# Fused weight products of the second attention: from sixteen steps ahead of the first attention to eight pieces inside it

## The reference

```
x = x + L0_attn(layernorm(x))   # 16 heads of 16, window of 64, a gated memory MLP and a SwiGLU FFN
x = x + L0_ffn(layernorm(x))    # relu MLP plus a weighted expert
x = x + L1_attn(layernorm(x))   # latent attention, 16 heads of 128
x = x + L1_ffn(layernorm(x))    # mixture of 16 experts, top 6, plus a shared one
```

```
c_kv = h @ W_DKV.T + b          # 64 wide
c_q  = h @ W_DQ.T + b           # 192 wide
q = c_q @ W_UQ.T + b ; k = c_kv @ W_UK.T + b ; v = c_kv @ W_UV.T + b    # 16 heads of 128
scores = q_h k_h^T / sqrt(128) ; out = concat_h(softmax(scores) v_h) @ W_O.T + b_O
```

## Time and profile before

| | |
|---|---|
| Time of before, median of 3 runs | 744.55 us (741.0 to 757.64) |
| Profiled execution, span | 757.9 us |
| PE busy | 691.1 us, 91% |
| DVE, ACT, POOL busy | 413.2, 329.3, 262.8 us |
| Chain that ended last: PE's share | 78% |
| Mean granted TensorE clock | 0.935 |

### The profile page before, as it was taken

One profiled execution on the slowest core, in us unless ns is written; L12 is line 12 of the kernel. 1 busy time (PEld: TensorE's weight loads), 2 busy tenths in 40 slices (PEclk: granted clock), 3 DMA queues, 4 the chain that ended last, 5 costly groups with the idle time before them and its releaser, 6 DMA issues.

```text
span 757.9 us, 13212 instructions
## 1 busy us (share of the span) xinstructions
PE 691.1 (91%) x5202; PEld 562.9 (74%) x5202; DVE 413.2 (55%) x870; ACT 329.3 (43%) x780; POOL 262.8 (35%) x340
## 2 busy tenths in 40 slices
PE   2979999899988699978689999799999999999997
PEld 1655767677777578866577777677888888888886
DVE  6566485833434766454836464566553454545455
ACT  2232535433533334444577687578442323232322
POOL 4313241602143650440732543235314334333400
PEclk9988889866889889998999999899999999999999
DMA  5322200000011220000200000000044433343201
GB/s 191 114 71 56 67 3 2 5 26 1 2 50 42 64 62 1 22 22 1 63 1 1 23 1 1 2 2 1 3 119 118 128 112 97 102 131 109 69 30 55
DMA packets 18636, 37.31 MB, mean 49 GB/s; under 512 B 2544, under 2 KB 4720, under 8 KB 18576
## 3 DMA queue, kind: packets, MB, share of 16 engines
q1 hardware_dynamic: 18576, 36.48, 16.0%
HBM read 35.19 MB, written 1.11 MB: 48 GB/s over the span
## 4 chain that ended last, share of the span: by engine, by line
PE 78%; DVE 9%; ACT 6%; POOL 3%; issue 3%; DMA 1%; DVEq 0%; SPq 0%; ACTq 0%; POOLq 0%
PE ps L632 50%; PE ps L945 4%; PE ps L957 4%; PE ps L751 3%; PE ps L935 3%; PE ps L775 3%; PE ps L710 2%; PE ps L654 2%; PE ps L658 1%; PE ps L640 1%; PE ps L725 1%; PE ps L649 1%; PE ps L693 1%; DVE st L1310 1%; DVE sml L1638 1%
## 5 line engine op out<-in xcount | busy, mean ns | idle before, releaser
L1841 POOL TENSOR_SCALAR PB<-PB,sml 128x256 f32<-128x256 f32 x128 | 60.2, 490 | 88.8 <-DVE sml L1655 88.8
L1151 ACT CAST VVh<-U 128x512 fp32r<-128x512 f32 x50 | 31.1, 621 | 114.3 <-DVE U L1512 106.6
L632 PE MATMUL ps<-ATh,wh 128*128 128x512 f32 x176 | 72.0, 409 | 3.6 <-POOL wl L1812 2.1
L632 PE MATMUL ps<-ATh,wl 128*128 128x512 f32 x176 | 70.9, 403 | 0.0
L632 PE MATMUL ps<-ATl,wh 128*128 128x512 f32 x176 | 70.8, 403 | 0.0
L1810 POOL TENSOR_SCALAR wh<-wr 128x768 fp32r<-128x768 f32 (+3 forms) x31 | 25.8, 833 | 129.0 <-PE ps L632 124.3
L1504 DVE TENSOR_TENSOR U<-U,ps 128x512 f32<-128x512 f32 x50 | 34.4, 688 | 62.5 <-PE ps L632 60.9
L1222 ACT ACTIVATE PB<-ps,sml 128x256 f32<-128x256 f32 x128 | 59.3, 487 | 8.8 <-DVE sml L1649 8.8
L1812 POOL TENSOR_TENSOR wl<-wr,wh 128x768 fp32r<-128x768 f32 (+3 forms) x31 | 56.0, 1806 | 2.6
L1516 DVE TENSOR_TENSOR VVl<-U,VVh 128x512 fp32r<-128x512 f32 x50 | 35.9, 718 | 37.1 <-ACT VVh L1151 37.1
L945 PE MATMUL ps<-SM,PB 128*128 128x128 f32 x256 | 37.8, 290 | 9.1 <-DVE QHl L1298 7.2
(11 more groups left out here) (294 smaller groups left out, 2050.0 us busy)
## 6 DMA issues: line engine op xcount, KB each, us to landing
wr<-in_w SPq DMA_DIRECT2D x32, 384.0 KB, 3.1
wr<-in_w SPq DMA_DIRECT2D x16, 321.0 KB, 2.9
CB<-weights_of_experts SPq DMA_DIRECT2D x16, 256.0 KB, 3.9
wr<-in_w SPq DMA_DIRECT2D x11, 256.0 KB, 2.6
CB<-weights_of_experts SPq DMA_DIRECT2D x8, 224.0 KB, 3.6
CB<-weights_of_experts SPq DMA_DIRECT2D x8, 192.0 KB, 3.7
CB<-weights_of_experts SPq DMA_DIRECT2D x8, 160.0 KB, 3.6
XO<-in_x SPq DMA_DIRECT2D x2, 512.0 KB, 4.7
```

Of the source, the lines that this page charges most:

```text
L632: t = x.matmul(o, a, b, start=first and i == 0 and c == 0, stop=last and i == n - 1 and c == 2, skip_group_check=skip)
L1151: x.copy((VV if run == "moe" else HH)[c][0][:, :], b[:, :]).then_inc(*mark("hi", "h", run, j, half))
L1841: t = x.tensor_scalar(p[:, c, :], p[:, c, :], m[:, 16 + c:17 + c], 1.0, ALU.mult, ALU.mult)
```

## The change

- `PROLOGUE`, `PERIOD` and `LAST` become one written list `FIRST`. With the `fuse`, `spin` and bias items taken out, the items of PE, ACT and DVE stand there in the same order as before, apart from `l0begin` and items that issue nothing. On POOL the splits of `wo` and `mem0` move from the end of the prologue to where `mem1` and `mem2` were split, so that four stand in a row.
- `fuse j` is now a piece of two heads, eight pieces in all. Pieces 0 and 1 stand among the scores of sequence 0; 2, 4 and 6 follow `expo 0 0`, `expo 1 0` and `expo 2 0`; 3, 5 and 7 follow `score 1 1`, `score 2 1` and `score 3 1`. Both halves k share one bank `fm`. ACT and DVE evacuate each piece right where it stands.
- The banks `fm` and `fn` come from the ring `w`, which has four banks from the start, and the scores have both pairs from the start. `l0begin` is gone.
- The 16 bias matmuls go. DVE adds up `bout` over the heads with 16 instructions (`biases j`), and one matmul with a column of ones sums over the partitions (`bias`).
- Both `spin` items (12 and 2 matmuls) go. The loads of `wr` wait for the bias sum too.

```diff
-        ring = {"w": Turns((6, 7)), "m": [Turns((2,)), Turns((3,))], "n": Turns((4,)), "S": Turns((8,))}
+        ring = {"w": Turns((4, 5, 6, 7)), "S": Turns((9, 8))}
...
+        def fuse(j):
+            bm, bn = fills(ring["w"], "fm", j), fills(ring["w"], "fn", j)
+            for i in range(2):
+                raw = raw_of(f"fuse{2 * j + i}")
+                uq, uk, uv, wo_ = raw[:, 0:256], raw[:, 256:321], raw[:, 321:385], raw[:, 386:642]
+                e.wait_ge(*loaded(f"fuse{2 * j + i}"))
+                x.matmul(bm[:, i * 65:i * 65 + 65], uq[:, 0:128], uk, start=True, stop=True)
+                t = x.matmul(bn[64 * i:64 * i + 64, 0:256], uv, wo_, start=True, stop=True)
+                if i:
+                    t.then_inc(*filled("fn", j))
+                t = x.matmul(bm[:, 130 + i * 65:130 + i * 65 + 65], uq[:, 128:256], uk, start=True, stop=True)
+            t.then_inc(*filled("fm", j))
+
+        def bias():
+            b = fills(ring["w"], "fb")
+            e.wait_ge(*at("biased", 15))
+            e.wait_ge(*at("ones"))
+            x.matmul(b[:, 0:256], ON[:, 16:17].to_broadcast([128, 128]), bout[:, :], start=True, stop=True).then_inc(
+                *filled("fb"))
...
+        def fuse(j):
+            lo_part(("fn", j), NTW[1][:, j, :], bank("fn", j)[:, 0:256], NTW[0][:, j, :])
+            (mh, rh), (ml_, rl) = fused_of(j)
+            vm, vr = fused_in(j)
+            e.wait_ge(*at("hi", "fm", j))
+            x.tensor_tensor(ml_, vm, mh.bitcast(F32), ALU.subtract)
+            x.tensor_tensor(rl, vr, rh.bitcast(F32), ALU.subtract).then_inc(*vacates("fm", j))
+
+        def biases(j):
+            for h in (2 * j, 2 * j + 1):
+                raw = raw_of(f"fuse{h}")
+                e.wait_ge(*loaded(f"fuse{h}"))
...
+                    e.wait_ge(*at("biased", h - 1))
+                    x.scalar_tensor_tensor(out=bout[:, :], in0=raw[:, 386:642], scalar=raw[:, 385:386], in1=bout[:, :],
+                                           op0=ALU.mult, op1=ALU.add).then_inc(*mark("biased", h))
...
                 if before.startswith("fuse"):
-                    e.wait_ge(*at("fused", int(before[4:])))
+                    e.wait_ge(*have("fm", int(before[4:]) // 2))
+                    e.wait_ge(*have("fn", int(before[4:]) // 2))
+                    e.wait_ge(*at("biased", int(before[4:])))
```

More of the change, by code:

```diff
@@ L142 @@
     _in[PART[_n]] = _n
-PROLOGUE = [
[15 rows of a table removed]
-]
-PERIOD = [
[9 rows of a table removed]
-]
-LAST = [
[6 rows of a table removed]
-    "mlpwide", "step@a mem 2 0", "split mem4", "oproj@p 5", "oproj@a 4", "step@a mem 3 0", "step@p mem 3 0",
[20 rows of a table removed]
-    "step@v ffn 2 1", "split exp", "split down", "ffnturn@v 0", "step@p ffn 3 1", "ffnturn@a 0", "step@a ffn 3 1",
[3 rows of a table removed]
-    "down ffn 4 1", "down ffn 5 1", "split proj", "latnorm 0", "latturn@v 0", "l1begin@v", "ffnmean@v 1", "latturn@a 0",
[13 rows of a table removed]
+FIRST = [
[61 rows of a table added]
+    "step@v ffn 1 1", "ffnnorm@a 0", "down@p ffn 1 1", "split@g exp", "step@a ffn 2 1", "step@v ffn 2 1", "ffnturn@p 0",
+    "split@g down", "step@p ffn 3 1", "ffnturn@a 0", "ffnturn@v 0", "step@a ffn 3 1", "down@p ffn 2 1", "step@v ffn 3 1",
[16 rows of a table added]
 ]
@@ L255, in split @@
             if LEFT[n] is not None and not done.get(LEFT[n]):
-                return
-            if n in ("wo", "mem0") and not state.get("fused"):
                 return
@@ L305, in mlp @@
         return tail[1]
-    for text in PROLOGUE:
-        kind, *a = text.split()
-        if kind == "split":
-            state["fused"] = True
-            split()
-        else:
-            item(kind, *map(int, a))
-    for b in range(3):
-        for text in PERIOD:
-            kind, d, k = text.split()
-            if kind == "spin":
-                item(kind, int(d))
-                continue
-            name, d, k = kind.partition("@")[0], int(d), int(k)
-            if b + d > 3 or b + d < 0 or d == 2 and b == 2:
-                continue
-            if name in ("project", "rope", "finish", "turnqk"):
-                item(kind, 2 * (b + d) + k)
-            elif name in ("headnorm", "turnmx"):
-                item(kind, b + d)
-            elif name not in ("weighed", "parted") or b + d >= 0:
-                item(kind, b + d, k)
-        if b == 1:
-            done["qkv0"] = done["qkv1"] = True
-            split()
-    for text in LAST:
+    for text in FIRST:
         kind, *a = text.split()
@@ L535, in half_cols, with fused_of, fused_in @@
         return slice(half * 512, half * 512 + 512)
+    def fused_of(j):
+        return [(m[:, :, j * 128:j * 128 + 128].rearrange("p k (h c) -> p k h c", c=64), r[:, :, 2 * j:2 * j + 2])
+                for m, r in zip(MTW, RTW)]
+    def fused_in(j):
+        v = bank("fm", j)[:, 0:260].rearrange("p (k h c) -> p k h c", k=2, c=65)
+        return v[:, :, :, 0:64], v[:, :, :, 64]
     def tile_cols(t):
@@ L641, in turn @@
             t.then_inc(*filled(*key))
-        def fuse(h):
-            raw = raw_of(f"fuse{h}")
-            uq, uk, uv, wo_ = raw[:, 0:256], raw[:, 256:321], raw[:, 321:385], raw[:, 386:642]
-            e.wait_ge(*loaded(f"fuse{h}"))
-            for k in range(2):
-                b = fills(ring["m"][k], "fm", h // 4, k) if h % 4 == 0 else bank("fm", h // 4, k)
-                t = x.matmul(b[:, (h % 4) * 65:(h % 4) * 65 + 65], uq[:, k * 128:(k + 1) * 128], uk, start=True, stop=True)
-                if h % 4 == 3:
-                    t.then_inc(*filled("fm", h // 4, k))
-            b = fills(ring["n"], "fn", h // 2) if h % 2 == 0 else bank("fn", h // 2)
-            lo = 64 * (h % 2)
-            t = x.matmul(b[lo:lo + 64, 0:256], uv, wo_, start=True, stop=True)
-            if h % 2:
-                t.then_inc(*filled("fn", h // 2))
-            b = fills(5, "fb") if h == 0 else bank("fb")
-            x.matmul(b[:, 0:256], raw[:, 385:386].to_broadcast([128, 128]), wo_, start=h == 0, stop=h == 15).then_inc(
-                *mark("fused", h))
+        def fuse(j):
[16 more added lines that the diff above has]
+                *filled("fb"))
         def turn1(half):
@@ L695, in turnqk @@
                 i.then_inc(*filled(key, t))
-        def l0begin():
-            ring.update(S=Turns((9, 8)), w=Turns((4, 5, 6, 7)))
-            for s in (vacated("fm", 3, 0), vacated("fm", 3, 1), vacated("fn", 7), vacated("fb")):
-                e.wait_ge(*s)
         def l0last():
@@ L893, in latconst @@
             e.wait_ge(*vacated("la", half, 2))
-            e.wait_ge(*vacated("fm", 3, 1))
+            e.wait_ge(*vacated("fm", 7))
             mm3(b[0:16, :], [((RTW[0][:, k, :], RTW[1][:, k, :]), (BT[0][:, k, sl], BT[1][:, k, sl]))
@@ L965, in l1out @@
             e.wait_ge(*vacated("lw", i))
+            e.wait_ge(*vacated("fn", j))
             for qt in range(2):
@@ L994, in spread @@
             p.then_inc(*filled("sp", half))
-        run(order, "p", {"spin": spin, "consts": consts, "fuse": fuse, "turn1": turn1, "project": project, "turnqk": turnqk, "l0begin": l0begin,
+        run(order, "p", {"spin": spin, "consts": consts, "fuse": fuse, "turn1": turn1, "project": project, "turnqk": turnqk, "bias": bias,
                     "score": score, "turnmx": turnmx, "expo": expo, "weigh": weigh, "oproj": oproj,
@@ L1029, in norm1 @@
                     x.copy(parts[k][0][:, 0:832], raw_of(f"qkv{k}")[:, 0:832]).then_inc(*mark("hi", f"qkv{k}"))
-        def fuse(h):
-            if h % 2:
-                hi_part(("fn", h // 2), NTW[0][:, h // 2, :], bank("fn", h // 2)[:, 0:256])
-            if h % 4 == 3:
-                j = h // 4
-                for k in range(2):
-                    v = bank("fm", j, k)[:, 0:260].rearrange("p (h c) -> p h c", c=65)
-                    e.wait_ge(*have("fm", j, k))
-                    x.copy(MTW[0][:, k, j * 256:j * 256 + 256].rearrange("p (h c) -> p h c", c=64), v[:, :, 0:64])
-                    x.copy(RTW[0][:, k, 4 * j:4 * j + 4], v[:, :, 64]).then_inc(*mark("hi", "fm", j, k))
+        def fuse(j):
+            hi_part(("fn", j), NTW[0][:, j, :], bank("fn", j)[:, 0:256])
+            (m, r), (vm, vr) = fused_of(j)[0], fused_in(j)
+            e.wait_ge(*have("fm", j))
+            x.copy(m, vm)
+            x.copy(r, vr).then_inc(*mark("hi", "fm", j))
         def turn(key, to, half, k, scale=None):
@@ L1376, in consts, with fuse, bias @@
                 *mark("slt"))
-        def fuse(h):
-            if h % 2:
-                j = h // 2
-                lo_part(("fn", j), NTW[1][:, j, :], bank("fn", j)[:, 0:256], NTW[0][:, j, :])
-            if h % 4 == 3:
-                j = h // 4
-                for k in range(2):
-                    v = bank("fm", j, k)[:, 0:260].rearrange("p (h c) -> p h c", c=65)
-                    mh, ml_ = (m[:, k, j * 256:j * 256 + 256].rearrange("p (h c) -> p h c", c=64) for m in MTW)
-                    e.wait_ge(*at("hi", "fm", j, k))
```

(22 more changed lines are left out.)

## The result

| | before | after |
|---|---|---|
| Timed median of the first comparison (4 runs each) | 748.84 us | 782.96 us (780.73 to 791.09) |
| Ratio, 95% interval | | 1.053 [1.041, 1.064] |
| Profiled execution, span | 757.9 us | 782.5 us |
| Mean granted clock | 0.935 | 0.915 |

The changed kernel is slower, by 34 us where 18.6 were predicted (763.0); 783 lies above the range, which ended at 775. The ratios leave out executions that were slow beside the others of the same kernel, the medians hold them all. On the two profiled executions the difference is 24.6 us, and it comes to 34 in the medians, since the profiled execution of before was a long one.

The account below looks back on a forecast made before the run. PE was taken to bound the periods, other engines' latency the emptied prologue. After 13.9 us gained, 5 were left at `project 4`; -5 + 10.4 + 4.8 + 4.5, 2.4 and 1.5 for clock gave +18.6: 763.0 us, range 748 to 775.

Parts of the forecast that it names:

- Milestones and waits: Start times from `project 0` to `project 4`, and new PE waits of 2.6, twice 3.1 and 1.85 us with named releasers.
- The half clock assumed for `project 0`: Prologue start: PE has done little by then, so the first projection takes 4.2 us at half clock.
- The first rival: New waits for DVE are hidden: 10.7 us fall away, +8, 752.5 us; chance 0.22.
- Pieces and waits at full clock: Periods and `bias`: 2.1 us per two-head piece, plus PE's waits for DVE and 0.53 for the bias matmul.
- theory B: From the experiments, not the prediction: pieces or waits cost more by themselves; no size or chance given.
- The timed median is 13 us lower, and I take the same difference for it: Whole run: profiled 776.5 us becomes a timed 763.0, as prologue and stretch behind `expo 0 0` both shorten.
- The 13.9 us gained: Prologue: without the fused products `expo 0 0` starts at 69.4 us against 83.29.
- "The clock", +2.4, +4.0 and +1.5: Half clock: 2.4 us on five pieces, 4 behind `expo 0 0`, 1.5 for falls behind the new waits.
- a new one often takes the place of an old one: Periods: clock falls behind four new waits mostly replace existing falls, so +1.5 us from a range of nothing to +10.
- the 1.28 us of idle time: Prologue of before: this PE idle time brought the fall to 1.2 GHz that lasted to 81.6 us.
- the named sign of being wrong: Periods: the forecast would be wrong if the clock there were far from 0.86.
- The clock rival: Each new wait lets the clock fall: 12 us in place of 1.5, 773.5 us; chance 0.18.

Follow-up runs that it names:

- Experiment 5: no_waits with useless matmuls in PE's idle stretches before `turnmx 0`, to keep the prologue's clock up: 759.7 us, ratio 1.022.
- experiment 1: The kernel before, unchanged, profiled a second time (the second execution of before): 750.2 us, span 748.3.
- experiment 12: The changed kernel once more, no edit, for the spread of its stages: 782.4 us.
- before_two_waits: The kernel before with one more PE wait ahead of `weigh 0 0` and of `weigh 1 0`: 762.5 us beside 749.4, ratio 1.016.
- small_pieces: no_waits with the matmuls of pieces 2 to 7 cut to 8 columns: 767.7 us, ratio 1.021.
- double_pieces: no_waits with the matmuls of pieces 2 to 7 each made twice: 789.4 us, ratio 1.059.
- no_waits: The changed kernel with DVE's parts of pieces 2, 3, 5 behind what PE waits for, and the bias matmul behind `oproj 3`: 757.1 us, ratio 1.019.
- spin_in_waits: The changed kernel with useless matmuls in PE's waits before `weigh 0 0`, `weigh 1 0` and the bias matmul, waits kept: 771.9 us, ratio 1.036.
- after_warm: The changed kernel with useless matmuls in all four new waits and in the prologue's idle stretches: 773.6 us, ratio 1.040.
- experiment 11: no_waits with pieces 0 and 1 moved into PE's early idle time, 2 and 3 where those stood: 761.8 us, ratio 1.017.
- bias_no_wait: The kernel before with PE's 16 bias matmuls replaced by DVE sums and one matmul, sums of heads 8 and 9 later: 754.0 us, ratio 1.010.

## Why the prediction was right or wrong

- **The bound, right.** PE sets the time of the periods, DVE and ACT that of the emptied prologue. Experiment 5 shows the second: clock 1.00 for 0.72 made 2.6 us.
- **Milestones and waits, right within some 2 us, one of them by luck.** `project 0` 18.7 (18.6), `score 0 1` 41.2 (42.6), `turnmx 0` 64.8 (67), `project 4` 82.9 (82.8). The last is two misses that cancel: `expo 0 0` came at 67.1 and not at 69.4, and the stretch behind it took 15.8 us and not 13.4, since all of it ran at 0.50 and not the first 9 us alone. The half clock assumed for `project 0` was wrong too: it was 1.00 from 18 to 28 us. The waits: 2.79 (2.6), twice 3.30 (3.1), 2.13 (1.85), each with the releaser named. The first rival, that DVE hides them, is out.
- **Pieces and waits at full clock, right.** The prediction's terms up to `turnmx 3` are six pieces of 2.1, the waits of 2.6, twice 3.1, 0.6 and 1.85, and 0.53 for the bias matmul: 24.4 us. Measured: 104.9 - 81.8 = 23.1, or 24.5 with the half wait put back. That leaves nothing for theory B.
- **"The timed median is 13 us lower, and I take the same difference for it": failed.** The 13.9 us gained were counted against a prologue in which the last four heads ran at half clock. In the second execution `expo 0 0` comes at 73.5 in before and 67.1 after, 6.4 us. The reasoning that the stretch behind it would be shorter too did not hold: its clock was 0.72 in both profiles of after. Of the gain 7.5 us were not there. The change cost 34.1 us by the medians where 18.6 were predicted, and of these 15.5 us that are missing this is the first half; another 4.3 us between 763.0 and 783.0 are the median of before, 748.84 in this comparison and 744.55 when the prediction was made.
- **"The clock", +2.4, +4.0 and +1.5: mis-sized.** Together 7.9 us; measured 14.9 in the periods, which is 7 more, the second half. Over whole runs the median loss grew by some 30 (34 to 65); the prologue's part of it, 11, costs little, since PE waits there, and the few us left lie behind the periods, in part by chance (experiment 12). Against the prediction's "a new one often takes the place of an old one", taking the waits away gave 25.8 us for 11.5, 19.6 of them in the periods. And its other premise, that the 1.28 us of idle time brought the fall behind them, is not enough: in experiment 1 the same stretch has no fall behind it. That the clock would be near 0.86 in the periods was the named sign of being wrong: it was 0.79. The clock rival (773.5, chance 0.18) was right in kind and still 9 us short, since it was built on the same gain in the prologue.
- **The rule for idle gaps.** The changed kernel lost more clock with its waits than without them (11 us back by filling three of them). The Trainium skill, page TensorE: Matmul & The Clock Gate, section on HAM oscillation, has idle gaps between bursts throttle the clock once per gap. The gaps of its example are longer, 3 to 5 us, so it does not price gaps of 2.1 to 3.3 us. What the runs show agrees in kind for the changed kernel. For before_two_waits the medians agree (9 us more lost for two waits) and its profile does not. Three things lie outside of the rule: the 1.28 us gap that had a fall behind it once and once not, and small_pieces and double_pieces, which lose some 13 to 17 us more than no_waits with about 3 us more of idle PE, spread over many short stretches.
- **Open.** Of the 14.9 us of clock in the periods idle PE accounts for about 9: no_waits, spin_in_waits and after_warm all come down to a loss of 19 to 20. The remaining 6 (before has 13.4) are not explained. Part may be the low clock that the emptied prologue leaves (experiment 11), but with a warm prologue 18.8 were still lost (experiment 5). Neither idle time nor the columns of the pieces alone order the kernels. Why the prologue of before ran at two speeds is open as well.

## What to carry to other kernels

Take the time of before from several executions before you count a gain against one stage of a single profile: a stage that ran at half clock by chance looks like something to win. Multiply span by mean clock, for both kernels: it separates work from clock and was steady to about 1% where the time was not to 2.5%. It misleads in a stage that PE does not bind, where a higher clock looks like more work (experiment 13). Work that is moved from a stage bound by another engine into one where PE is full pays its whole length there, and the four waits of 2 to 3 us that it brought to PE cost more than their length here: 19.6 us in the periods for 11.5, and 25.8 by the medians of whole runs. So put the evacuation behind what PE waits for.

## What the runs showed of the hardware

- The granted clock stayed at 1.2 GHz under a PE without idle time. Two windows of 4 us of the changed kernel (length, PE, loads, DVE, ACT, POOL, PEclk, DMA share, GB/s):

```profile
68.00:72.00 4.00, 4.00 (x28) 3.10 (x26) 0.00 (x0) 1.00 (x3) 0.00 (x0) 0.50 0.01 2
80.00:84.00 4.00, 4.00 (x31) 3.58 (x28) 0.91 (x2) 2.27 (x3) 0.00 (x0) 0.50 0.00 0
```

- The pattern of the clock often repeats where the instructions do (periods of 52.20 and 52.37, 46.76 and 46.80, 34.23 and 34.24 us in two executions), and yet the prologue of one kernel, before, took 56.7 or 66.6 us. The second attention's units took about 168.3, 171.3 or 172.8 us in all 17 profiles. The third period of before took 32.4 to 32.9 us at 0.68 or 0.69 in the six other profiles that have it unchanged, and in bias_no_wait, with the same list of items, 24.8:

```profile
142.97:167.77 24.80, 23.89 (x391) 17.78 (x387) 16.06 (x19) 11.53 (x21) 9.99 (x12) 0.93 0.09 23
```

- Less work did not make a kernel faster: small_pieces took out matmul columns worth 6 us at full clock, lost 13 to 17 us more to the clock than no_waits, and has the ratio 1.021 beside 1.019.
